# Pooling steps taken earlier on VectorE, exponentials ahead of the squares on ScalarE, one token fetched sooner on GpSimd, in a two-layer batch kernel

## The reference

```python
# layer 0, HID 2048, OUT 512 = 384 shared + 128 of the sample's expert
h = gelu(einsum('bnd,hd->bnh', x, fc1_w) + fc1_b)
shared = einsum('bnh,sh->bns', h, fc2_w) + fc2_b
expert_x = einsum('bnh,bph->bnp', h, experts_w[indices]) + experts_b[indices][:, None, :]
x = x + concatenate([shared, expert_x], -1)
# layer 1
scores = einsum('bsa,a->bs', tanh(einsum('bsd,da->bsa', x, W1) + b1), v)
masked = where(mask, scores[:, None, :], -1e30)      # mask: l <= j, l >= j or l != j
pooled = einsum('bjl,bld->bjd', softmax(masked), x) / cnt
x = x + pooled
```

## Time and profile before

| | |
|---|---|
| median of 3 runs | 1350.99 us |
| the profiled execution, its own time | 1351.38 us |
| its span | 1349.6 us |
| PE busy | 1302.4 us, 97% |
| DVE busy | 1075.9 us, 80% |
| ACT busy | 966.7 us, 72% |
| POOL busy | 261.8 us, 19% |
| mean DMA rate | 101 GB/s |

### The profile page before, as it was taken

How to read it: one execution, slowest core, us unless ns; L and a number is a source line. 1 busy time by engine, 2 the same in 40 slices (tenths; PEclk the granted TensorE clock), 3 DMA queues, 4 the chain that set the end, 5 groups by cost and what they waited for, 6 DMA issues and landing times.

```text
span 1349.6 us, 25573 instructions
## 1 busy us (share of the span) xinstructions
PE 1302.4 (97%) x9849; PEld 960.2 (71%) x9849; DVE 1075.9 (80%) x2092; ACT 966.7 (72%) x1764; POOL 261.8 (19%) x380
## 2 busy tenths in 40 slices
PE   9999999999999999999999999999999999999998
PEld 4458476577867778677786877868678686777856
DVE  7988898668869687796877868688596886968798
ACT  5768868586786867768577685877868678686772
POOL 0000101022212122222122211222112321222202
PEclk9999999999999999999999999999999999999999
DMA  8540223136344363534536254363543634436206
GB/s 293 163 111 18 63 75 83 40 90 122 87 116 93 104 135 71 122 77 119 115 86 126 64 133 95 94 126 71 125 92 95 121 86 112 93 103 125 66 15 121
DMA packets 73884, 136.43 MB, mean 101 GB/s; under 512 B 9746, under 2 KB 34210, under 8 KB 71330
## 3 DMA queue, kind: packets, MB, share of 16 engines
q0 software_dynamic: 28032, 56.63, 24.4%
q1 hardware_dynamic: 45154, 77.38, 17.2%
q10 hardware_dynamic: 576, 0.79, 0.2%
HBM read 45.65 MB, written 18.87 MB: 48 GB/s over the span
## 4 chain that ended last, share of the span: by engine, by line
PE 78%; DVE 11%; ACT 5%; DMA 3%; issue 2%; SPq 0%; POOL 0%; DVEq 0%; ACTq 0%; POOLq 0%
PE ps L547 13%; PE ps L549 13%; PE ps L548 13%; PE ps L649 12%; PE ps L660 5%; PE ps L657 4%; PE ps L636 3%; PE ps L637 3%; PE ps L638 3%; DMA hl<-hl 2%; ACT L1199 1%; DVE hl L1731 1%; DVE hh L1731 1%; ACT space L1202 1%; ACT g L1034 1%
## 5 line engine op out<-in xcount | busy, mean ns | idle before, releaser
L547 PE MATMUL ps<-xh,w1h 128*128 128x256 f16 x960 | 261.8, 273 | 1.5
L548 PE MATMUL ps<-xl,w1h 128*128 128x256 f16 x960 | 261.7, 273 | 0.0
L549 PE MATMUL ps<-xh,w1l 128*128 128x256 f16 x960 | 261.7, 273 | 0.0
L1034 ACT ACTIVATE g<-ps,b1s,ds 128x512 f32<-128x512 f32 x240 | 173.4, 773 | 65.4 <-PE ps L549 65.4
L547 PE MATMUL ps<-xh,ch 128*128 128x256 f16 x720 | 196.3, 273 | 1.5
L549 PE MATMUL ps<-xh,cl 128*128 128x256 f16 x720 | 196.2, 273 | 0.0
L548 PE MATMUL ps<-xl,ch 128*128 128x256 f16 x720 | 196.2, 273 | 0.0
L1619 DVE SCALAR_TENSOR_TENSOR hl<-g,ix,hh 128x512 f16<-128x512 f32 x243 | 175.9, 745 | 3.1
L1008 ACT ACTIVATE hh<-g,ix 128x512 f16<-128x512 f32 x243 | 161.6, 718 | 0.0
L649 PE MATMUL ps<-hh,w 128*128 128x512 f16 x576 | 134.1, 379 | 0.0
L2657 POOL DMA_DIRECT2D g<-space x30 | 36.9, 1230 | 487.9 <-DMA g<-space 444.5
(11 more groups left out here) (364 smaller groups left out, 3080.4 us busy)
## 6 DMA issues: line engine op xcount, KB each, us to landing
space<-in_xT SPq DMA_DIRECT2D x62, 256.0 KB, 3.2
g<-space SPq DMA_DIRECT2D x60, 256.0 KB, 2.6
er<-in_ew SPq DMA_DIRECT2D x15, 1024.0 KB, 4.8
out<-space SPq DMA_DIRECT2D x60, 256.0 KB, 3.2
space<-space POOLq DMA_DIRECT2D x52, 256.0 KB, 3.3
hl<-hl POOLq DMA_DIRECT2D x24, 512.0 KB, 7.9
g<-space POOLq DMA_DIRECT2D x30, 256.0 KB, 3.9
g<-g POOLq DMA_DIRECT2D x30, 256.0 KB, 4.0
```

Source lines behind the costliest of these rows:

```text
L547: mm(to, wh, mh, start=i in (1, 5) and c == 0, stop=False, skip_group_check=True)
L548: mm(to, wh, ml, start=False, stop=False, skip_group_check=True)
L549: m = mm(to, wl, mh, start=False, stop=c == 1, skip_group_check=True)
L1034: act(in_two(g_of(b, k)), src, ACT.Gelu, bias=b1s[:, k:k + 1], scale=ds1[:, b % 2, p:p + 1]).then_inc(gelu_done)
```

## The change

On DVE the numbers of pooling steps are redistributed. For samples 4 to 14 `takes` holds one step fewer or more here and there (16 in all, 17 before), and `late` now has four places with 1, 0, 1, 0 steps; a new place stands between `add_second(b, 7)` and `expert_low(b, 0)`. A paired sample now begins with 27 steps done and has the next pooling's steps 8 and 9 done in the last `cycle`, step 10 between `low` 10 and 11, and step 11 at the new place. Later come `pool(2)` (12, 13), `pool(4)` (14 to 17), `pool(6)` (18 to 23), `pool(2)` (24, 25) and `pool(2)` (26, 27). `third_sum` moves ahead of `bounds`. Sample 3 takes 20 steps in its `takes` and then joins this pattern; the last sample takes four steps fewer and reaches the same point.

On ScalarE `one_way_exponentials` moves ahead of `e_squares`, that is right behind `split_expert_high(b, 3)`, and `inverses` moves to where it stood. On GpSimd the first part of `mend`, which reads the lone token's place, copies it and scales it, becomes `fetch` and is called in `sum_quarters` between `third_low_sum` and the addition of T2. On TensorE `score(b)` comes one product earlier in the paired opening, ahead of `product3(n, 0)`, and `sum1` EXPERT no longer waits for the evacuation of the second chunk; ScalarE's first copy of that sum has the wait.

```diff
             if v == EXPERT:
-                e.wait_ge(x2_done, nth_chunk(b, 1))
                 e.wait_ge(el_done, nth_chunk(b, 3))
...
             product4(n, 0)
+            score(b)
             product3(n, 0)
-            score(b)
             product7(n, 1)
...
         def first_of_sum(b, v):
             e.wait_ge(s_done, nth_product(b, v, 1))
+            if v == EXPERT:
+                e.wait_ge(x2_done, nth_chunk(b, 1))
...
             split_expert_high(b, 3)
             if b == LAST:
                 break
+            if paired(b):
+                one_way_exponentials(b - 1)
             e_squares(b + 1)
...
                 first_of_sum(b, EXPERT)
-                one_way_exponentials(b - 1)
+                inverses(b - 1)
                 split_x_high(b + 1, X11)
+                split_x_high(b + 1, X21)
                 second_of_sum(b, STATIC)
-                split_x_high(b + 1, X21)
                 split_x_high(b + 1, T3)
                 second_of_sum(b, EXPERT)
                 split_x_high(b + 1, T1)
                 third_of_sum(b, STATIC)
-                inverses(b - 1)
...
-            takes = ((0, 3, 1), (1, 1, 1), (1, 2, 1), (1, 1, 1), (1, 1, 1), (0, 0, 0))
-            late = (0, 0, 0)
+            takes = ((0, 1, 1), (1, 1, 1), (1, 1, 1), (1, 1, 1), (1, 1, 1), (0, 1, 1))
+            late = (1, 0, 1, 0)
...
+            elif b == 3:
+                takes = ((0, 3, 1), (1, 1, 1), (1, 2, 1), (1, 1, 1), (1, 1, 1), (1, 1, 1))
             elif b == LAST:
-                takes, late = ((0, 3, 1), (1, 1, 1), (1, 2, 1), (0, 0, 0), (0, 0, 0), (1, 0, 0)), (1, 1, 2)
+                takes, late = ((0, 1, 1), (1, 1, 1), (1, 1, 1), (0, 0, 0), (0, 0, 0), (1, 0, 0)), (1, 1, 0, 1)
...
             add_second(b, PAIRS - 1)
+            pool(late[2])
...
                 pool(2)
+                third_sum(b)
                 bounds(b + 1)
-                third_sum(b)
-                pool(3)
+                pool(4)
...
-                pool(7)
+                pool(6)
...
-                pool(3)
+                pool(2)
                 attention_low(b)
...
             if paired(b - 1):
                 third_low_sum(b - 1)
+            if b > 2:
+                fetch(b - 2)
             e.wait_ge(*combined_by(b, T3))
```

More of the change, by code:

```diff
@@ L2265, in vector_program @@
         for b in range(1, B):
-            takes = ((0, 3, 1), (1, 1, 1), (1, 2, 1), (1, 1, 1), (1, 1, 1), (0, 0, 0))
-            late = (0, 0, 0)
+            takes = ((0, 1, 1), (1, 1, 1), (1, 1, 1), (1, 1, 1), (1, 1, 1), (0, 1, 1))
+            late = (1, 0, 1, 0)
             if b == 1:
-                takes, late = ((0, 0, 0),) * 5 + ((1, 1, 1),), (2, 2, 2)
+                takes, late = ((0, 0, 0),) * 5 + ((1, 1, 1),), (2, 2, 0, 2)
             elif b == 2:
-                takes, late = ((0, 3, 1), (1, 1, 1), (1, 2, 1), (1, 2, 0), (1, 2, 0), (2, 2, 0)), (1, 1, 3)
+                takes, late = ((0, 3, 1), (1, 1, 1), (1, 2, 1), (1, 2, 0), (1, 2, 0), (2, 2, 0)), (1, 1, 0, 3)
+            elif b == 3:
+                takes = ((0, 3, 1), (1, 1, 1), (1, 2, 1), (1, 1, 1), (1, 1, 1), (1, 1, 1))
             elif b == LAST:
-                takes, late = ((0, 3, 1), (1, 1, 1), (1, 2, 1), (0, 0, 0), (0, 0, 0), (1, 0, 0)), (1, 1, 2)
+                takes, late = ((0, 1, 1), (1, 1, 1), (1, 1, 1), (0, 0, 0), (0, 0, 0), (1, 0, 0)), (1, 1, 0, 1)
             for c, (one, two, three) in zip(range(2, PAIRS), takes):
@@ L2300, in vector_program @@
             expert_low(b, 1)
-            pool(late[2])
+            pool(late[3])
             low(b, 12)
@@ L2608, in add_other, with fetch @@
             eng.dma_start(out[b, :, c, 0:S - 1], pooled_rows(b, c)[1][:, 1:S], accum_op=ALU.add).then_inc(second_added, 16)
[L2610 to L2615, removed]
+        tokens_at = {}
+        def fetch(n):
+            done, is_c, lone, held = pool_value(n, 0), e2[:, n:n + 1], cell(n, 19), cell(n, 34, 4)
             e.wait_ge(pool_step, done + 2)
@@ L2619, in mend @@
                 e.wait_ge(s_step, s_value(n, ALL_ADDED))
-            at = eng.value_load(cell(n, 8)[0:1, :].bitcast(i32), min_val=0, max_val=S - 1)
+            at = tokens_at[n] = eng.value_load(cell(n, 8)[0:1, :].bitcast(i32), min_val=0, max_val=S - 1)
             eng.tensor_copy(held, flat(xr[:, n % XB, :, bass.ds(at, 1)])).then_inc(mend_step)
@@ L2624, in mend @@
             eng.tensor_scalar(held, held, lone, is_c, ALU.mult, ALU.mult).then_inc(mend_step)
+        def mend(n):
+            at = tokens_at[n]
+            done, is_c = pool_value(n, 0), e2[:, n:n + 1]
+            inverse = cell(n, 23, 2)
+            share, rest, both, one = cell(n, 38), cell(n, 39), cell(n, 40, 4), cell(n, 44, 4)
             e.wait_ge(pool_step, done + 16)
```

## The result

The changed kernel takes 1422.65 us (median of 4 runs, 1422.36 to 1424.74) against 1350.95: a ratio of 1.0534, 95% interval 1.0516 to 1.0552. That is 71.7 us more, where 61 were forecast. Its profiled execution has a span of 1420.8 us.

The account below looks back on a forecast made before the run. PE, busy 97% of the span, was taken to bound the kernel. 5.5 us for `sum5` less 0.4 for the score is 5.1 us in each of 12 samples, 61 us: 1412 us, range 1378 to 1434.

Parts of the forecast that it names:

- second stall: At `sum6`: PE idles 1 us for the high half; the low half, set by the `third_low_sum` DMA, is 5.1 us late.
- Step 11 at the head of the queue: On DVE ahead of the low parts: 10.3 us of idle time for the exponentials; last low part 6.4 us late.
- First stall: At `sum1` STATIC: a new wait of 2.5 us for the last low part.
- Third stall: At `sum5`: 5.1 + 0.4 = 5.5 us late, and with it the rest of the corrections.
- The score: `score(b)` earlier in the paired opening: ACT's `keep_score` and Gelu about 0.5 us sooner, -0.4 us a sample (0 to -0.8).
- The moved steps, the fetch, the moved `x2_done` wait: Steps moved into the first matrix: 0 (-0.1 to +0.3 us a sample); `fetch` on POOL: 0 (0 to +1); `x2_done` wait: 0.
- The table load: On ACT before the exponentials: 1.29 us from load to first exponential; by the page's figure the result some 17 us higher.
- the DMA isn't last: At `second_sum(hl)`: POOL's DMAs don't keep their distance, so 2.5 us a sample, 1381 us; chance 0.14.
- GpSimd's chain gets longer still: DMA times at their upper end and `fetch` in the way: +1.5 us a sample, 1430 us; chance 0.11.
- the clock falls: PE at 1.2 GHz for the 8 us from `sum6` to `sum5`: about 100 us more, 1510 us; chance 0.03.
- The other side, exponentials in time: `exp_done` comes by about 798.7, so the stalls at `sum6` and `sum5` go: -4.5 us a sample, 1297 us; chance 0.05.

Follow-up runs that it names:

- first two experiments: Changed kernel with step 11 alone moved behind the low parts: 1320.17 us; changed kernel with step 11 behind `expert_low` 0 and 1: 1407.40 us.
- the filled idle time: Changed kernel with 24 matmuls, product unread, added on TensorE between the high and low half of `sum6` STATIC: 1423.55 us, ratio 1.0532.
- first experiment: Changed kernel with step 11 alone moved behind the low parts, to the pool call behind `expert_sum2`: 1320.17 us, ratio 0.977.

## Why the prediction was right

The direction and the mechanism were right, and the range (1378 to 1434) held the time; it was 10.7 us short, 5.1 us a sample for a measured 6.0. Samples stand 88.57 us apart (step 11 starts at 305.88 and at 1280.12 us, 11 samples later). Part of the agreement is luck: SyncE's issues of samples 4 to 8 are 87.63 to 88.09 us apart, where 87.6 was forecast, but two errors of about half a microsecond cancel there (the second stall, below), and samples 9 to 14 are 88.8 to 89.7 apart.

- **Step 11 at the head of the queue.** Forecast 10.3 us of idle time, measured 10.40. The first two experiments show that this is the cause: without it the change is a gain, and the one pair of low parts that was taken from behind it gives its own time back.
- **First stall.** Forecast 2.5, measured 2.60.
- **Second stall.** The high half was forecast at 1 us and is 0.77 in sample 9, though only six samples have it (6.3 us in all). For the low half DVE was to wait 2.5 us for the DMA; it waits 4.52 in sample 9 and 3.7 on average (44.7 us in 12). The term that I sized wrong is the distance from T3's addition to T1's, taken over at 4.4 us from the trace. It is now 4.8 to 6.5 us, 5.65 on average. The cause of that distance, which I couldn't name, shows itself in the landing times: in sample 9 T3's addition needs 6.1 us and T1's follows 0.4 us behind its landing (4.0 and 0.4 before), and it is so in every sample. `third_low_sum` itself landed sooner than I took, 5.9 us for 6.3. Together +0.9 us a sample, nearly the whole difference; the slow clock (at most 2.8 us in all) and what the score gained beyond its forecast (2.0 us in all) roughly cancel.
- **Why T3's addition lands later.** The traces point at two things, and no run tests either. In every sample SyncE's four plain DMAs are now issued in one run of 3.86 us instead of 5.01, and the packets of the addition start 2.5 us behind its issue, right behind the last of theirs, instead of 1.8: it lands in 4.5 to 4.6 us in samples 3 to 7, and in 3.9 to 4.0 before (in all samples but the third, which is slower in both respects). In samples 9 to 14 it takes 5.7 to 6.1 us, and there a 16 KB packet of the queue that the profile calls `instruction` runs for 0.9 to 1.1 us beside the addition; in samples 3 to 7 none does until it has landed; in sample 8, where it takes 5.1 us, one begins 4.56 us behind the issue. Sample 9 (from 840.21 us, to the landing) has the first two lines, sample 5 (from 488.64) the third and no line of q8:

```profile
q8 instruction: 1, 0.02, 1.0%
...
g<-space POOLq DMA_DIRECT2D x1, 256.0 KB, 6.1
...
g<-space POOLq DMA_DIRECT2D x1, 256.0 KB, 4.5
```

In the 36 samples of this kernel, of step 11 between the low parts and of the filled idle time, the 17 with such a packet begun 1.9 to 4.1 us behind T3's issue have 5.99 to 6.52 us from T3's addition to T1's, and the 19 without have 4.79 to 5.55. By this the packet accounts for about 8 of the 10.7 us missed (an estimate: six samples at 6.31 us on average for 5.00 in the other six). Where such packets fall wasn't in the working at all.

- **Third stall.** Forecast 5.5 us of lateness with a wait of `sum5` that stays near 2. The 0.4 us of it that DVE's own list adds are 0.28 (9.78 us from `second_sum(hl)` to `first_sum(hh)` in eight samples, 9.50 before). But the wait has nearly gone (5.2 us in all): PE came late by itself, at half clock. With the clock kept up it is back, 23.2 us.
- **The score.** Forecast -0.4, measured alone -0.57.
- **The moved steps, the fetch, the moved `x2_done` wait at nothing.** The first experiment has all of them and comes to 1320 us, where the same working gave 1323. So together they cost nothing that shows; one by one they weren't measured.
- **The table load.** It went by the row's 1.29 us: step 11 starts 2.57 us behind the start of the load (831.90 to 834.47), as before. The drain that the Trainium skill, ScalarE: Activation LUTs, What ACT_TABLE_LOAD costs, adds to each switch is not seen here either.

The rivals: that the DMA isn't last fell (44.7 us of wait for it). That GpSimd's chain gets longer still, which I gave 0.11 and 1430 us, came half true, but not by the causes that I named: `third_low_sum` landed in 5.8 to 6.6 us, not 7.3, and `fetch` stands behind it. That the clock falls came true, which I gave 0.03; it cost at most 2.8 us (an estimate: the 0.72, 0.82, 0.53 and 0.70 us by which `sum5` came late) and not 100, since I had priced it as if nothing else were late. The Trainium skill, TensorE: Matmul & The Clock Gate, Why this matters for your kernels, was right that such gaps bring the half clock; the row that bears on it is 0.52 of the full clock behind 4.69 us of idle time. The other side, exponentials in time, is what the first experiment makes by another way: not by earlier exponentials but by a later step 11.

The change as a whole is then, if its parts simply add up: -6.9 for the score, -23.9 for the exponentials, the fetch and the steps around them, +102.5 for one step in front of eight low parts.

Left open: whether the `instruction` packet is what slows T3's addition, or only comes with it. A run that moves those packets and nothing else would tell.

## What to carry to other kernels

Before a waiting instruction is moved up in an engine's list, work out when its semaphore comes, and list everything that stands behind it and is needed sooner: the move costs what the wait holds back. Idle time of that engine is room for the instruction only if its semaphore comes within it. And where an engine's lateness reaches a chain of DMAs issued one behind the other, count the chain from its first link; when one wait is removed, look for the next one within a microsecond or two before booking the gain.

## What the runs showed of the hardware

- TensorE's granted clock, at 2.4 GHz throughout the kernel before, was 1.2 GHz for 7 us behind 4.69 us without a matmul in the changed kernel. Behind the stall of 2.60 us at `sum1` it fell in six samples of that kernel and stayed up in the six others. In the kernel with the filled idle time it fell twice behind 1.74 us (once 0.51 from 515.5 to 519.0 us), while behind the two stalls of 1.4 us a sample of the kernel before it never did. So in these traces the length of one gap alone doesn't decide it.
- Two accumulating DMAs of GpSimd with 256 KB each weren't issued side by side in the kernels before and after: the second went out 0.3 to 0.4 us behind the first one's landing, while `third_low_sum` followed the second after 0.74 us, long before that landed.
- The landing of one and the same DMA (T3's addition) took 3.9 to 4.9 us before, and 4.5 to 6.1 us in the changed kernel. The 5.7 us and more came only where a 16 KB packet of the `instruction` queue, 0.9 to 1.1 us long, ran beside it.
